# Householder steps below 128 in the form of the later ones: pieces in PSUM, an unmasked column for PE

## The chip, the core and the metric

The kernel runs on one core of one Trainium2 chip. The metric is the device time of one execution in microseconds, the median of several. All times stated here are microseconds unless marked ns.

## What is computed

Two residual layers on x (64 x 256 x 256), float32 throughout.

```python
# layer 0
h = relu(layernorm(x))                      # per batch element 256 nodes x 256 features
h = relu((adj*adj) @ (h @ W1))              # 256 -> 512
h = relu((adj*adj) @ (h @ W2))              # 512 -> 1024
x = x + (adj*adj) @ (h @ W3)                # 1024 -> 256
# layer 1
deg = adj.sum(0) + adj.sum(1) - diag(adj)
L_norm = d[:, None] * (diag(deg) - adj) * d[None, :]     # d = deg ** -0.5
_, U = eigh(L_norm)                         # once, 256 x 256
h = relu(layernorm(x))
x = x + U @ (relu((U.T @ h) @ W1 + b1) @ W2 + b2)
```

## The kernel before

The work falls into three parts. The batch is taken in 32 pairs of two elements for layer 0. Beside it runs the eigenvalue problem of the 256 x 256 matrix `A`: a reduction to tridiagonal form by 254 Householder steps, then bisection and eigenvectors on VectorE. Layer 1 follows when `U` is there.

`A` lies in SBUF as two blocks of 128 rows (`A[:, 0, :]`, `A[:, 1, :]`). A Householder step k takes column k of `A`, makes a reflector from it and updates the columns from k + 1 on (`rest`), 255 - k of them. Steps 0 to 127 involve both blocks of rows and are written by `householder`; from 128 on only the lower block is left, and `householder_one` writes them. The order of every engine is written out by hand, and the engines signal each other by counting semaphores. One step of `householder` goes like this:

- PE turns the masked column `xc` (two blocks) into a row that stands in all 128 partitions of the PSUM bank `p_x` (`step_x`, recorded on L1365). Below I call this turn X.
- VectorE copies the row to SBUF (`xr`, L874). It multiplies `A` by it and sums (L877, result `pc`). ScalarE meanwhile squares and sums `xr` (L611) and takes the root (L613).
- From the root VectorE makes `beta` (L882 to L888), then `qcol` (L890), `h_` (L892), the reflector `v` (L893), and after the reciprocal of `h_` the scaled `vn` (L900), `qn` (L902) and the negated inverse (L903). GpSimd saves `beta` and `v` (L460, L461).
- PE turns `qcol` into the row `p_q` (`step_q`, L1365 too). I call this turn Q.
- VectorE makes the first `col` (L906), the sum of a product (L909), the first update of either block of `A` (L865), `w` (L914), the second `col` (L918), which is the next column complete, the second update of block 0 (L869), the mask `xc` (L923), which lets PE go on, and the second update of block 1.

`householder_one` does the same for one block and differs in form: it subtracts where the other adds, its `beta` has one operation instead of two after the reciprocal but each of them waits for the one before, its second update reads the row where PE left it in PSUM (alternating `ps[0]` and `ps[2]`), and PE turns `col` itself: the mask follows behind the second update, for `v` of the next step. All of VectorE's operations count up `house_v`, HOUSE = 22 a step, and `done(i)` waits until i of the step have ended.

Between the turns X and Q, and between Q and the next X, PE does the matrix products of a pair of layer 0. `GROUPS` says which pairs go with how many steps: pairs 0 to 3 take 11 steps each, pairs 4 to 17 take 12, pairs 18 to 20 take 14. `beside` spreads a pair's products over the steps, 0.54 of each step's share between X and Q. A group is a hardware loop over its pairs on PE, ScalarE and GpSimd. Step 128 falls on the beginning of pair 11. ScalarE evicts the products; in a step it does the square and the root first. GpSimd makes scalars of the layer norm, in steps 116 to 123 the sums of weights (`sum_of_weights`, L496) that pairs from 11 on need, and at the end of each pair two additions of x to the result (`add_x`, L487), 128x512 each.

## Time and profile before

| | |
|---|---|
| runs, median of 3 | 2407.68 us (2406.26 to 2408.15) |
| profiled execution | 2405.8 us |
| its span | 2404.1 us |
| PE busy | 2332.5 us, 97% of the span |
| VectorE busy | 1981.1 us, 82% |
| ScalarE busy | 1011.2 us, 42% |
| GpSimd busy | 858.2 us, 36% |
| chain that ended last | PE 70%, VectorE 24% |
| mean granted TensorE clock | 0.995 |

The steps 0 to 127 take the first 791 us of the span, the steps from 128 on the time up to 1421 us, and then VectorE's bisection follows. PE's busy share is that of operations whose ends are modelled and that overlap, so a short idle time between two of them is hardly seen in it; where PE loses time is better read from the distances between its turns. Rows of a timeline show the start, the duration, the engine, the line, the operation with its output and inputs, and in brackets the idle time before it and what ended it. DVE is VectorE, ACT is ScalarE, POOL is GpSimd, and PEld is the loading of weights on PE.

### The profile page before, as it was taken

The page shows a single profiled execution, that of the slowest core. Times are in us where ns is not written, and L with a number is a line of the kernel's source. Part 1 is how long each engine was busy: PE and PEld are TensorE (multiplying, and loading weights), DVE is VectorE, ACT ScalarE, POOL GpSimd, SP SyncE. Part 2 cuts the span into 40 slices and gives each one's busy share as a digit, 9 for nine tenths or more (in the row PEclk, how much of TensorE's full clock was granted, in tenths as well). Part 3 has the DMA queues.
Part 4 walks back from the last instruction along what each step waited for, and adds up shares of the span by engine and source line. Part 5 has one row for each costly group of instructions (what it writes and reads, how often), then busy time and mean ns, then how long its engine had stood idle before and what let it go on. Part 6 is the DMA issues. An engine that isn't in the chain of part 4 may idle for free.

```text
span 2404.1 us, 44229 instructions
## 1 busy us (share of the span) xinstructions
PE 2332.5 (97%) x11228; PEld 1920.7 (80%) x11228; DVE 1981.1 (82%) x10140; ACT 1011.2 (42%) x2428; POOL 858.2 (36%) x1582
## 2 busy tenths in 40 slices
PE   6999999999999999999999999999999997999999
PEld 4788877777887777888877778887788886889998
DVE  6888888888888888877788889799999994447776
ACT  3333333333333444444444444444444443235554
POOL 1111111111112554444444455445545444243332
PEclk9999999999999999999999999999999998999999
DMA  2000000000000000000000000000000001014443
GB/s 99 27 27 27 9 27 18 27 27 27 27 9 27 19 27 27 27 26 27 27 27 27 27 27 27 27 10 27 26 26 26 27 27 35 18 44 135 132 131 110
DMA packets 90001, 89.72 MB, mean 37 GB/s; under 512 B 5376, under 2 KB 89088, under 8 KB 89856
## 3 DMA queue, kind: packets, MB, share of 16 engines
q1 hardware_dynamic: 89856, 88.23, 11.5%
q14 instruction: 108, 0.88, 0.1%
q8 instruction: 37, 0.61, 0.1%
HBM read 54.66 MB, written 33.55 MB: 37 GB/s over the span
## 4 chain that ended last, share of the span: by engine, by line
PE 70%; DVE 24%; issue 2%; POOL 2%; ACT 2%; SPq 0%; DMA 0%; POOLq 0%; DVEq 0%; ACTq 0%
PE ps L1451 30%; PE ps L1423 25%; PE ps L1629 9%; DVE ps L1064 6%; PE ps L1365 4%; DVE ahead L1067 3%; DVE shared L1148 3%; DVE ps L1145 2%; DVE ahead L1043 2%; PE ps L1639 1%; DVE negs L1070 1%; POOL hid2T L518 1%; PE ps L1576 1%; DVE A L865 1%; DVE A L869 0%
## 5 line engine op out<-in xcount | busy, mean ns | idle before, releaser
L460 POOL COPY Eb<-sc 128x1 f32 (+1 forms) x254 | 46.7, 184 | 850.0 <-DVE v L893 614.1
L1423 PE MATMUL ps<-agg2T,w 128*128 128x256 f32 x1408 | 325.1, 380 | 0.5
L1451 PE MATMUL ps<-w,hid2T 128*128 128x256 f32 x1344 | 307.2, 381 | 11.8 <-ACT hid2T L671 11.8
L1451 PEld LDWEIGHTS ps<-w,hid2T 128*128 128x128 f32 x1344 | 247.9, 190 | 57.1 <-ACT hid2T L671 21.9
L1423 PEld LDWEIGHTS ps<-agg2T,w 128*128 128x128 f32 x1408 | 257.8, 190 | 33.2 <-ACT agg2T L650 3.3
L611 ACT ACTIVATE squares<-xrow_sb 128x256 f32<-128x256 f32 (+5 forms) x128 | 47.7, 372 | 432.3 <-DVE xrow_sb L874 432.3
L1064 DVE RECIPROCAL ps<-ahead 128x40 f32<-128x40 f32 (+1 forms) x768 | 218.4, 331 | 0.1
L1451 PE MATMUL ps<-w,aggT 128*128 128x512 f32 x336 | 151.9, 597 | 13.1 <-ACT aggT L664 13.1
L1423 PE MATMUL ps<-w,hid2T 128*128 128x256 f32 x704 | 162.9, 379 | 0.0
L1451 PE MATMUL ps<-agg2T,w 128*128 128x256 f32 x672 | 156.0, 379 | 0.0
L1451 PE MATMUL ps<-hid2T,xin 128*128 128x256 f32 x672 | 155.5, 380 | 0.0
L487 POOL TENSOR_TENSOR xr<-xr,res 128x512 f32<-128x512 f32 x64 | 84.8, 1325 | 193.5 <-ACT res L664 171.5
L1451 PE MATMUL ps<-weightT,hid 128*128 128x256 f32 x672 | 152.1, 379 | 0.0
L1067 DVE SCALAR_TENSOR_TENSOR ahead<-ps,ne,ahead 128x40 f32<-128x40 f32 (+1 forms) x768 | 147.2, 224 | 0.0
L1451 PEld LDWEIGHTS ps<-weightT,hid 128*128 128x128 f32 x672 | 125.8, 191 | 24.1 <-issue 8.7
L1423 PEld LDWEIGHTS ps<-w,hid2T 128*128 128x128 f32 x704 | 129.5, 190 | 15.3
L1451 PEld LDWEIGHTS ps<-hid2T,xin 128*128 128x128 f32 x672 | 125.4, 190 | 17.2
L1451 PEld LDWEIGHTS ps<-agg2T,w 128*128 128x128 f32 x672 | 124.6, 190 | 17.9
L664 ACT ACTIVATE hid2T<-ps 128x512 f32<-128x512 f32 x168 | 99.1, 590 | 82.8 <-PE ps L1451 82.6
L613 ACT ACTIVATE root_s<-root_s,tiny 128x1 f32<-128x1 f32 x254 | 74.8, 295 | 131.5 <-DVE prods L947 125.1
L1451 PEld LDWEIGHTS ps<-w,aggT 128*128 128x128 f32 x336 | 62.6, 192 | 78.5 <-issue 63.6
L671 ACT ACTIVATE hid2T<-hid2T 128x512 f32<-128x512 f32 x168 | 101.6, 623 | 33.6 <-POOL hid2T L518 31.2
(387 smaller groups left out, 5700.0 us busy)
## 6 DMA issues: line engine op xcount, KB each, us to landing
xl<-in_x_dram SPq DMA_DIRECT2D x64, 256.0 KB, 2.9
xr<-in_x_dram SPq DMA_DIRECT2D x64, 256.0 KB, 2.9
x_dram<-xr SPq DMA_DIRECT2D x64, 256.0 KB, 2.3
xin<-x_dram SPq DMA_DIRECT2D x64, 256.0 KB, 2.8
out_dram<-xin SPq DMA_DIRECT2D x64, 256.0 KB, 2.2
w<-in_L_gnn_W_dram SPq DMA_DIRECT2D x1, 2048.0 KB, 9.4
w<-in_L_gnn_W_dram SPq DMA_DIRECT2D x1, 1024.0 KB, 11.4
w<-in_L_gnn_W_dram SPq DMA_DIRECT2D x1, 512.0 KB, 4.1
```

Of the source, the lines that this page charges most:

```text
L487: pool.tensor_tensor(xres[:, j, :, :], xres[:, j, :, :], res[:, j, :, :], ALU.add).then_inc(x1_ready, 1)
L613: act.activation(root_s[:, 1:2], root_s[:, 0:1], ACT.Sqrt, bias=tiny[:, 0:1]).then_inc(root, 1)
L664: act.activation(dst.rearrange("p a n -> p (a n)"), ring[i % 4][:, :], ACT.Relu if stage == "hid" else ACT.Copy).then_inc(evac, 1)
L671: act.activation(block_, block_, ACT.Relu).then_inc(fin, 1)
L1043: ins = dve.tensor_tensor(piv[g % 2][:, 0:n, d, :], diag.unsqueeze(2).to_broadcast([P, n, W]), pts.unsqueeze(1).to_broadcast([P, n, W]), A ...
L1064: inverse_made[d] = at(dve.reciprocal(inverse[:, d, :], here[:, d, :]))
L1067: pivot_made[d] = at(dve.scalar_tensor_tensor(there[:, d, :], inverse[:, d, :], ne2[:, off:off + 1], there[:, d, :], ALU.mult, ALU.add))
L1148: dve.scalar_tensor_tensor(Qfb[:, i + 1, lane], inverse_at(i)[:, lane], ne2[:, off:off + 1], Qfb[:, i + 1, lane], ALU.mult, ALU.add).then_ ...
L1365: ins = pe.transpose(dst[:, P * b:P * b + P], col(b).to_broadcast([P, P]), ident[:, 0, 0:P])
L1423: ins = pe.matmul(dst, a, b, start=start, stop=stop)
L1451: ins = pe.matmul(dst, a, b, start=start, stop=stop)
L1629: ins = pe.matmul(dst, a, b, start=start, stop=stop)
```

## The change

The steps below 128 are written by a new `householder_two`, which is `householder_one` for two blocks. `at_row(p_here, i)` is a piece of two columns in the same PSUM bank as the row, behind its 256 columns. There lie the sums `p_` (was `pc`), `vh` (was `vn`), `w_` (was `w`) and the next masked column. The bank alternates with k, `ps[0]` for even k, `ps[2]` for odd k. PE turns `col` unmasked. `xr` is cleared at the start and its element k + 1 at the end of each step, so that the part before `rest` stays zero for ScalarE's square. The mask is made of two operations of one column, behind both second updates. Since the bank has to be known where a loop's body is written, an odd number of steps allows one pair a group, and the two groups of 11 steps become four. In `householder_one` only the masked column moves to PSUM.

```diff
-        GROUPS = [(0, 2, 11, 0.54), (2, 4, 11, 0.54), (4, 6, 12, 0.54), (6, 8, 12, 0.54), (8, 10, 12, 0.54),
-                  (10, 11, 12, 0.54), (11, 14, 12, 0.54), (14, 18, 12, 0.54), (18, 21, 14, 0.54)]
+        GROUPS = [(0, 1, 11, 0.54), (1, 2, 11, 0.54), (2, 3, 11, 0.54), (3, 4, 11, 0.54), (4, 6, 12, 0.54),
+                  (6, 8, 12, 0.54), (8, 10, 12, 0.54), (10, 11, 12, 0.54), (11, 14, 12, 0.54), (14, 18, 12, 0.54),
+                  (18, 21, 14, 0.54)]
...
+            def at_row(p_here, i):
+
+                return p_here[:, N + NB * i:N + NB * i + NB]
...
+                p_, vh, w_, x_next, x_now = (at_row(p_here, 0), at_row(p_here, 1), at_row(p_here, 2), at_row(p_here, 3),
+                                             at_row(p_last, 3))
...
+                def second_update(b):
+                    return dve.scalar_tensor_tensor(A[:, b, rest], p_here[:, rest], w_[:, b:b + 1], A[:, b, rest],
+                                                    ALU.mult, ALU.subtract)
...
+                at(dve.tensor_copy(xr[:, rest], p_here[:, rest]))
+                for b in range(NB):
+                    ins = dve.scalar_tensor_tensor(prods[:, b, rest], A[:, b, rest], 1.0, p_here[:, rest],
+                                                   ALU.mult, ALU.mult, accum_out=p_[:, b:b + 1])
...
+                done(4)
+                at(dve.tensor_scalar(twice, inv_len, square, length, ALU.mult, ALU.add))
+                done(5)
+                dve.wait_ge(v_saved, k + 1)
+                at(dve.tensor_scalar(beta, twice, half, None, ALU.mult))
...
+                at(dve.tensor_scalar(vh, v[:, :], inv_h, None, ALU.mult))
+                dve.wait_ge(q_ready, k + 1)
+                at(dve.tensor_scalar(qn[:, :], qcol[:, :], inv_h, None, ALU.mult))
+                done(11)
+                dve.wait_ge(qrow, k + 1)
+                at(dve.scalar_tensor_tensor(prods[:, NB - 1, rest], p_q[:, rest], inv_h, xr[:, rest],
+                                            ALU.mult, ALU.mult, accum_out=uq))
+                at(dve.scalar_tensor_tensor(col[:, :], vh, p_q[:, here:here + 1], A[:, :, here], ALU.mult, ALU.subtract))
+                done(14)
+                at(first_update(0))
...
+                done(16)
+                dve.scalar_tensor_tensor(col[:, :], w_, head, col[:, :], ALU.mult, ALU.subtract).then_inc(col_ready, 1)
+                at(second_update(0))
+                done(17)
+                at(second_update(1))
+                dve.wait_ge(col_ready, k + 2)
+                for b in range(NB):
+                    ins = dve.tensor_scalar(x_next[:, b:b + 1], col[:, b:b + 1], below[:, b, here:here + 1], None, ALU.mult)
+                at(ins)
+                at(dve.memset(head, 0.0), HOUSE - 20)
...
-            def step_x(k, bl, s):
+            def step_x(k, bl, bank):
                 pe.wait_ge(col_ready, k + 1)
-                row(p_turn[s % 2] if len(bl) == 1 else p_x, lambda b: (col if len(bl) == 1 else xc)[:, b:b + 1], bl).then_inc(xrow, 1)
+                row(bank, lambda b: col[:, b:b + 1], bl).then_inc(xrow, 1)
```

VectorE, from the sum of the product to the copy of the next step, in step 0 before:

```order
L906 SCALAR_TENSOR_TENSOR col<-vn,ps,A 128x2
L909 SCALAR_TENSOR_TENSOR prods,sc<-ps,sc,xrow_sb 128x255
L865 SCALAR_TENSOR_TENSOR A<-ps,vn,A 128x255
L914 SCALAR_TENSOR_TENSOR w<-vn,sc,qn 128x2
L865 SCALAR_TENSOR_TENSOR A<-ps,vn,A 128x255
L918 SCALAR_TENSOR_TENSOR col<-w,xrow_sb,col 128x2
L869 SCALAR_TENSOR_TENSOR A<-xrow_sb,w,A 128x255
L923 TENSOR_TENSOR xc<-col,below 128x2
L869 SCALAR_TENSOR_TENSOR A<-xrow_sb,w,A 128x255
L874 COPY xrow_sb<-ps 128x256
```

and the same stretch now:

```order
L913 SCALAR_TENSOR_TENSOR prods,sc<-ps,sc,xrow_sb 128x255
L915 SCALAR_TENSOR_TENSOR col<-ps,A 128x2
L876 SCALAR_TENSOR_TENSOR A<-ps,A 128x255
L919 SCALAR_TENSOR_TENSOR ps<-ps,sc,qn 128x2
L876 SCALAR_TENSOR_TENSOR A<-ps,A 128x255
L922 SCALAR_TENSOR_TENSOR col<-ps,xrow_sb,col 128x2
L880 SCALAR_TENSOR_TENSOR A<-ps,A 128x255 x2
L928 TENSOR_SCALAR ps<-col,below 128x1 x2
L930 MEMSET xrow_sb 128x1
L885 COPY xrow_sb<-ps 128x254
```

The first `col` has gone behind the product, the mask from between the two second updates to behind them, and a clearing has come in before the next copy. PE waits for L923 before and for L922 now.

VectorE, from the root to `qcol` in the same step before:

```order
L882 RECIPROCAL sc<-root_s 128x1
L884 TENSOR_TENSOR sc<-root_s,sc 128x1
L885 TENSOR_TENSOR sc<-root_s,sc 128x1
L888 SCALAR_TENSOR_TENSOR sc<-sc 128x1
L890 SCALAR_TENSOR_TENSOR qcol<-A,sc,pc 128x2
```

and now:

```order
L892 RECIPROCAL sc<-root_s 128x1
L894 TENSOR_SCALAR sc<-sc,root_s 128x1
L897 TENSOR_SCALAR sc<-sc 128x1
L899 SCALAR_TENSOR_TENSOR qcol<-A,sc,ps 128x2
L900 TENSOR_SCALAR sc<-ps,sc 128x1
```

One operation is gone from this stretch, and each of those left reads the result of the one before.

## Rows read from the trace of the kernel before

**Rows 1.** Waits of the whole span: engine, line, waited for; total us, times, longest.

```profile
PEld ps L1365 <- DVE xc L923: 41.9, 76, 1.2
```

**Rows 2.** Timeline of PE: turns Q and X, 11-step pair, then 12-step pair.

```profile
246.73 0.38 PE L1365 MATMUL ps<-ident,qcol 128*128 128x128 f32 x2
...
249.54 0.38 PE L1365 MATMUL ps<-ident,xc 128*128 128x128 f32 x2
...
252.79 0.38 PE L1365 MATMUL ps<-ident,qcol 128*128 128x128 f32 x2
...
615.58 0.38 PE L1365 MATMUL ps<-ident,xc 128*128 128x128 f32 x2
...
618.83 0.38 PE L1365 MATMUL ps<-ident,qcol 128*128 128x128 f32 x2
...
621.20 0.38 PE L1365 MATMUL ps<-ident,xc 128*128 128x128 f32 x2
```

**Rows 3.** Timeline of VectorE and PE's turns: the step k = 54.

```profile
357.74 0.43 PE L1365 MATMUL ps<-ident,xc 128*128 128x128 f32 x2
358.28 0.38 DVE L874 COPY xrow_sb<-ps 128x212 f32<-128x212 f32 x1 [0.25 <-PE ps L1365]
...
359.52 0.16 DVE L882 RECIPROCAL sc<-root_s 128x1 f32<-128x1 f32 x1
...
360.10 0.22 DVE L890 SCALAR_TENSOR_TENSOR qcol<-A,sc,pc 128x2 f32<-128x2 f32 x1
...
361.03 0.22 DVE L902 TENSOR_SCALAR qn<-qcol,sc 128x2 f32<-128x2 f32 x1
361.03 0.38 PE L1365 MATMUL ps<-ident,qcol 128*128 128x128 f32 x2
...
361.52 0.23 DVE L906 SCALAR_TENSOR_TENSOR col<-vn,ps,A 128x2 f32<-128x2 f32 x1 [0.22 <-PE ps L1365]
...
362.81 0.21 DVE L918 SCALAR_TENSOR_TENSOR col<-w,xrow_sb,col 128x2 f32<-128x2 f32 x1
362.94 0.42 DVE L869 SCALAR_TENSOR_TENSOR A<-xrow_sb,w,A 128x201 f32<-128x201 f32 x1
363.28 0.16 DVE L923 TENSOR_TENSOR xc<-col,below 128x2 f32<-128x2 f32 x1
...
363.49 0.43 PE L1365 MATMUL ps<-ident,xc 128*128 128x128 f32 x2
```

**Rows 4.** Timeline at the end of a 12-step pair, step k = 55.

```profile
366.78 0.38 PE L1365 MATMUL ps<-ident,qcol 128*128 128x128 f32 x2
...
368.39 1.26 POOL L487 TENSOR_TENSOR xr<-xr,res 128x512 f32<-128x512 f32 x1 [1.55 <-ACT res L650]
368.56 1.11 DVE L918 SCALAR_TENSOR_TENSOR col<-w,xrow_sb,col 128x2 f32<-128x2 f32 x1
...
370.04 1.51 POOL L487 TENSOR_TENSOR xr<-xr,res 128x512 f32<-128x512 f32 x1 [0.38 <-ACT res L650]
370.14 0.43 PE L1365 MATMUL ps<-ident,xc 128*128 128x128 f32 x2 [0.81 <-DVE xc L923]
```

**Rows 5.** Timeline of VectorE and GpSimd in step 119.

```profile
741.01 1.27 POOL L496 TENSOR_TENSOR adj_sb<-w,xin 128x512 f32<-128x512 f32 x1
741.05 1.25 DVE L902 TENSOR_SCALAR qn<-qcol,sc 128x2 f32<-128x2 f32 x1
```

**Rows 6.** The masks, steps below 128 and from 128: durations min/median/max ns, first and last start.

```profile
L923 DVE TENSOR_TENSOR xc<-col,below x128: 147/158/1250, 32.2 to 791.2; 128x2 f32<-128x2 f32 x128
L985 DVE TENSOR_SCALAR xc<-col,below x126: 202/212/217, 796.7 to 1420.6; 128x1 f32<-128x1 f32 x126
```

**Rows 7.** Timeline of VectorE in step 128: reciprocal of the length, `qcol`.

```profile
792.86 0.16 DVE L953 RECIPROCAL sc<-root_s 128x1 f32<-128x1 f32 x1
...
793.62 0.27 DVE L960 TENSOR_SCALAR qcol<-A,sc,pc 128x1 f32<-128x1 f32 x1
```

**Rows 8.** Timeline of VectorE at the start: a clearing of one column.

```profile
0.87 0.06 DVE L816 MEMSET tiny<- 128x1 f32 x1 [0.87 <-PEq L1686]
```

**Rows 9.** Updates of 205 columns by form, 336 to 350 us: total us, mean ns.

```profile
L865 DVE SCALAR_TENSOR_TENSOR A<-ps,vn,A 128x205 f32<-128x205 f32 x2 | 0.9, 428 | 0.0
...
L869 DVE SCALAR_TENSOR_TENSOR A<-xrow_sb,w,A 128x205 f32<-128x205 f32 x2 | 0.8, 432 | 0.0
```

More of the change, by code:

```diff
@@ L371, in completed @@
             return [i for i, m in slot if m == (2 if UNITS[i][0] == "hid" else SIZE[UNITS[i][0]]) - 1]
+        for first, last, steps, _ in GROUPS:
+            assert last - first == 1 or steps % 2 == 0
         @block.sync
@@ L858, in at @@
                     ins.then_inc(house_v, n)
-                half, inv_len, h_, beta, inv_h, minus_inv_h, scaled, uq = (sc[:, i:i + 1] for i in range(1, 9))
+                half, inv_len, h_, beta, inv_h, _, twice, uq = (sc[:, i:i + 1] for i in range(1, 9))
                 square, length = root_s[:, 0:1], root_s[:, 1:2]
-                head = xr[:, here:here + 1]
+                head, top = xr[:, here:here + 1], p_here[:, here:here + 1]
+                p_, vh, w_, x_next, x_now = (at_row(p_here, 0), at_row(p_here, 1), at_row(p_here, 2), at_row(p_here, 3),
+                                             at_row(p_last, 3))
@@ L879, in householder @@
                 at(ins)
-                at(dve.tensor_scalar(half, head, 0.0, 0.5, ALU.is_ge, ALU.subtract))
+                at(dve.tensor_scalar(half, top, 0.0, 0.5, ALU.is_ge, ALU.subtract))
                 dve.wait_ge(root, k + 1)
                 at(dve.reciprocal(inv_len, length))
-                done(3)
-                at(dve.tensor_tensor(scaled, length, half, ALU.mult))
-                at(dve.tensor_tensor(uq, square, half, ALU.mult))
+                done(4)
+                at(dve.tensor_scalar(twice, inv_len, square, length, ALU.mult, ALU.add))
@@ L895, in householder @@
-                done(8)
-                at(dve.tensor_scalar(head, head, beta, None, ALU.add))
                 at(dve.reciprocal(inv_h, h_))
-                done(10)
+                at(dve.tensor_scalar(top, top, beta, None, ALU.add))
+                done(9)
                 dve.wait_ge(v_ready, k + 1)
-                at(dve.tensor_scalar(vn[:, b0:NB], v[:, b0:NB], inv_h, -1.0, ALU.mult, ALU.mult))
+                at(dve.tensor_scalar(vh, v[:, :], inv_h, None, ALU.mult))
                 dve.wait_ge(q_ready, k + 1)
-                at(dve.tensor_scalar(qn[:, b0:NB], qcol[:, b0:NB], inv_h, -1.0, ALU.mult, ALU.mult))
@@ L940, in householder_one @@
                 head, top = xr[:, here:here + 1], p_here[:, here:here + 1]
-                x_, v_, vh, w_, q_, qh, col_, p_ = (t[:, b:NB] for t in (xc, v, vn, w, qcol, qn, col, pc))
+                v_, vh, w_, q_, qh, col_, p_ = (t[:, b:NB] for t in (v, vn, w, qcol, qn, col, pc))
+                x_now, x_next = at_row(p_last, 3)[:, b:NB], at_row(p_here, 3)[:, b:NB]
                 done(0)
@@ L984, in householder_one @@
                 dve.wait_ge(col_ready, k + 2)
-                at(dve.tensor_scalar(x_, col_, below[:, b, here:here + 1], None, ALU.mult), HOUSE - 17)
+                at(dve.tensor_scalar(x_next, col_, below[:, b, here:here + 1], None, ALU.mult), HOUSE - 17)
+            link(dve.memset(xr[:, :], 0.0))
+            link(dve.tensor_tensor(at_row(p_turn[1], 3), A[:, :, 0], below[:, :, 0], ALU.mult))
             dve.wait_ge(house_v, 1)
-            dve.tensor_tensor(xc[:, :], A[:, :, 0], below[:, :, 0], ALU.mult).then_inc(col_ready, 1)
+            dve.tensor_copy(col[:, :], A[:, :, 0]).then_inc(col_ready, 1)
+            dve.wait_ge(col_ready, 1)
             for (first, last, steps, _), k0 in zip(GROUPS, FIRST_STEP):
@@ L1483, in _ @@
             for k in TAIL:
-                step_x(k, range(NB - 1, NB), k - TAIL[0])
+                step_x(k, range(NB - 1, NB), p_turn[k % 2])
                 step_q(k, range(NB - 1, NB))
```

59 lines of the change are left out of this document (16 added, 43 removed).

## Prediction

> **What bounds the kernel now.** I read the waits first, then PE's two row turns in each Householder step, then VectorE's part of one step. The longest thing PE's loads wait for in these steps is VectorE's masked column: 41.9 us in 76 waits [rows 1]. That is not the loss, since PE is often still multiplying while a load waits. The loss shows in the distances between the turns. I call the turn of the column X, the turn of `qcol` Q. In a step of an 11-step pair X to Q takes 3.25 us and Q to X 2.81 us [rows 2]; there PE is never short of work (both distances stay the same while VectorE's operations get narrower). In a 12-step pair the floor of the second distance is 2.37 to 2.38 us, as the narrow step near 618 us shows [rows 2], so PE's floors are 6.05 us a step in 11-step pairs and 3.25 + 2.37 = 5.62 in 12-step pairs. (k is the step; the width of the rest of A is 255 - k, 201 at k = 54.)
>
> At k = 54 a 12-step step takes longer than its floor: X to Q 3.29 (357.74 to 361.03) and Q to X 2.46 (361.03 to 363.49), in all 5.75 [rows 3]. The 0.08 in the second half is VectorE's chain, which ends with `xc`, 0.06 before PE's turn; the 0.05 in the first half is PE starting again after having stood still.
>
> The largest loss is at the end of each pair. There GpSimd adds x to the result (1.26 us and 1.51), and one VectorE operation that begins beside it takes 1.11 us instead of 0.21; Q to X is then 3.36 (366.78 to 370.14) [rows 4]. The longest `xc` is 1.25 where its median is 0.158 [rows 6]. The operations so stretched read two tensors from SBUF; those that read one of them in PSUM keep their length. In the steps 116 to 123 GpSimd sums weights, and there `qn`, two columns from SBUF to SBUF, takes 1.25 us; [rows 5] show one of the eight.
>
> **The change part by part.** k below 128 only; what PE multiplies for the features is the same.
>
> (1) **Ends of pairs.** With the pieces in PSUM, everything that VectorE does beside GpSimd's addition has at most one SBUF tensor: both kinds of update, the column steps, the products. The mask is now 128x1; this form in the later steps has a maximum of 217 ns over 126 executions, although GpSimd makes the same additions there [rows 6]. I take the stretch as gone. Each of the seven 12-step ends loses 3.36 - 2.38 = 0.98 now, plus the 0.05 of the restart. The excess shrinks with the width, since the chain that the stretch is added to shortens, to about 0.8: 7 x 0.97 = 6.8 us. In the four 11-step ends the stretch of 1.25 - 0.16 = 1.09 is added to a chain that has 0.3 to spare (2.81 against 2.5 of VectorE): 4 x 0.85 = 3.4. Together 10.2 us. Bounds: 0, if another operation is caught, and 10.5.
>
> (2) **The column reaches PE earlier.** Now from the start of the second `col` operation to PE's turn: 363.49 - 362.81 = 0.68 [rows 3]. After the change nothing stands between: its 0.21 and 0.06 of signal, 0.27. Against this, the first `col` now follows the product sum and the first update waits for it: 0.23 + 0.04 in place of an issue gap of 0.14, so +0.13. Net 0.28 at 202 columns. Q to X by VectorE becomes 2.46 - 0.28 = 2.18, under PE's 2.38. Ordinary 12-step steps so lose 0.08 + 0.05 at k = 54; by three width-dependent operations at 1 ns a column the 0.08 was 0.11 at k = 44 and is gone at about k = 81. A mean of 0.105 over some 32 steps is 3.4 us. In the second step of each pair PE has less work in the second half and waits for VectorE in all pairs: 10 x (0.25 + 0.05) = 3.0 us.
>
> (3) **VectorE's own loop gets longer**, and this is what takes something back. Between copy and `qcol`: the reciprocal to `qcol` takes 0.58 now (359.52 to 360.10) and 0.76 in the form that is taken over (792.86 to 793.62) [rows 3, 7], +0.18. After the last column operation two updates, two masks and a clearing of `head` must end before the next copy: 0.13 + 2 x 0.34 for the updates, 2 x 0.13 for the masks (the next operation starts 0.08 before the end of one, 362.94 + 0.42 to 363.28; a mask takes 0.212 [rows 6]), 0.06 for the clearing [rows 8], 0.04 for its signal: 1.17. The loop at 202 columns: copy to `qcol` 1.82 + 0.18; `qcol` to `qn` 0.93 and 0.14 to the product sum; from there to the second `col` 1.29 + 0.13; then 1.17. In all **5.66 us**. Seven width-dependent operations make it 0.007 a step: 5.73 at k = 44, 5.62, the floor, at k = 60, and 6.03 at k = 1 against 6.05. So VectorE becomes the bound of about 17 steps by 0.055 in the mean: -0.9 us. In the second and fourth step of a pair PE waits for an eviction that ScalarE makes after the root, and so after the copy; the copy is up to 0.15 later in the first two 12-step pairs: -0.6 us.
>
> (4) **Steps 116 to 123.** `qn` is still a 128x2 operation from SBUF to SBUF and still begins 0.58 after `v`, some 0.04 behind GpSimd's sum [rows 5]. It stays stretched, so VectorE's loop is the bound in these steps, and its change counts in full: +0.18, +0.13, -0.06 (the negated inverse is gone), -0.09 (1.05 for the tail against 0.55 + 0.05 + 0.54 by way of PE at 136 columns). +0.16 in six of the eight: -1.0 us.
>
> (5) **PSUM as a place for operands.** An update that reads its row in PSUM takes 428 ns, one that reads it in SBUF 432, at 205 columns [rows 9]. Pointers and accumulators in PSUM are not in the trace for this form; I bound them by 0 and by the 0.013 us that small operations differ, and take 0.07 a step over the 30 or so in which VectorE is at or near the bound: -2 us (at 0.1 and 40 steps -4).
>
> The Trainium skill, "VectorE: DVE Perf Modes", section "The TRN2 errata — SBUF-src ops pay a fixed extra latency per instruction", has a table in which a VectorE instruction costs 58 cycles plus its width from SBUF and 120 from PSUM, 65 ns more at 0.96 GHz; it speaks against this change. By it the eight or so operations moved would cost 0.5 us a step. The pair of [rows 9] disagrees with it by its whole amount, and the sum goes by the rows.
>
> (6) **At nothing:** copies of `rest` only (a few ns); the products that no longer wait for the copy (the root on ScalarE is later, 359.52 being its end); the four single groups in place of two loops. PE is fed in the same order, and a first pass through new code has shown no gap where groups change already. The start (clearing `xr`, two small operations) lies under the wait for weights.
>
> Steps from 128 on only move `x` to PSUM; the mask there ends well ahead of PE's row. From the end of the reduction on VectorE's eigenvalue chain begins earlier by what was gained, and I see nothing that would hold it.
>
> **Sum:** 10.2 + 3.4 + 3.0 - 0.9 - 0.6 - 1.0 - 2 = 12.1 us. The profiled execution took 2405.8 us (span 2404.1), so it would be 2393.7; it lies 1.9 under the median of 2407.68, for which I say **2396 us**. Its own range is 2391 to 2401: the small costs in (5) at zero or twice, the tail of (3) 0.05 off either way.
>
> **The rivals.**
> - *`qn` escapes in steps 116 to 123.* 0.04 us decides it [rows 5], and if VectorE is first, GpSimd waits only for its 0.22. Then these steps fall from 6.03 to near 5.62, which is 3.6 us more: 2392. For it: the small margin. Against: all eight were caught, and the distance from `v` to `qn` stays. The Trainium skill, "SBUF — State Buffer", section "Who interferes with whom", says of the shared pair that the first to issue holds it for its whole instruction. Chance 0.15.
> - *The loop is 0.14 longer than I make it* (masks and clearing do not overlap, or a wait costs more). Then VectorE bounds 35 to 40 steps and the gain halves: 2402. Chance 0.12.
> - *The pair ends stay stretched*, because another operation is caught, the clearing or a mask. Then 10.2 us mostly stay lost: 2405. Against: rows of the later steps. Chance 0.07.
> - *VectorE's loop becomes the bound everywhere, and the kernel slower.* Place: from the second `col` to the next copy, and each operation with a piece in PSUM. With 0.3 us more a step the loop is 5.96 at 202 columns and 6.33 at k = 1; over the steps 1 to 40 and 44 to 100 that costs some 20 us against the gains of 14: about 2415. Below +0.23 a step it is no loss. For it: ten operations change place and two are added. The table of the Trainium skill cited under (5) would give +0.5 a step and some 30 us beyond this. Against: [rows 9]. Chance 0.07.
>
> The chances: forecast 0.59, the rivals 0.15, 0.12, 0.07, 0.07. What this kernel's measurement can tell from no change is about 0.2%, 4.8 us: faster means below 2402.9. The forecast and the first rival lie there, and so does a third of the second. Faster 0.78, same 0.15, slower 0.07. The range that leaves out the last rival and the far end of the first: 2390 to 2405.
>
> **What the new profile would show.** (1) right: no VectorE operation of 1.1 us or more at a pair's end, Q to X there 2.8 and 2.4. (2): PE's turn 0.27 after the second `col` begins. (3): copy-to-copy 5.73 at k = 44 and 5.62 from k = 60 on; a copy 0.7 to 0.8 after X where it was 0.54. (4): `qn` at 1.25 us eight times, steps of 6.1 to 6.2. Wrong would be: copy-to-copy over 6.05 in the first pairs, an update over 0.45 at 205 columns, or long operations elsewhere beside GpSimd.

## The result, and the profile after

| | before | after |
|---|---|---|
| median of 7 runs | 2407.68 us (2405.16 to 2409.19) | 2398.58 us (2395.62 to 2399.31) |
| profiled execution | 2405.8 us | 2395.62 us |
| its span | 2404.1 us | 2393.9 us |
| VectorE busy | 1981.1 us | 2016.5 us |
| chain that ended last, PE / VectorE | 70% / 24% | 61% / 30% |

The ratio is 0.996 with the 95% interval [0.9949, 0.9971], so the changed kernel is faster by some 9.1 us. I forecast 2396 (own range 2391 to 2401). The profiled execution was the fastest of its seven; its span is 10.2 us shorter, against the 12.1 of my sum.

The sum by kinds of steps, read from PE's turns in both traces (time before minus time after, added up over the steps named; a minus is a loss):

| steps | X to Q | Q to X | together |
|---|---|---|---|
| last of a pair, three of the 11-step pairs | 0.00 | 2.49 | 2.49 |
| last of a pair, all seven 12-step pairs | 0.1 | 6.5 | 6.5 |
| first step, six 12-step pairs | 0.34 | 0.26 | 0.60 |
| fifth to eleventh step, six 12-step pairs | 0.89 | 0.92 | 1.81 |
| second step, six 12-step pairs | -1.04 | 1.23 | 0.19 |
| third step, six 12-step pairs | -0.01 | 0.16 | 0.15 |
| fourth step, six 12-step pairs | -1.32 | 0.17 | -1.15 |
| second step, three 11-step pairs | -0.01 | 0.65 | 0.64 |
| third step, three 11-step pairs | -1.14 | 0.01 | -1.13 |
| 116 to 123 | -0.53 | -0.31 | -0.84 |
| all of pair 0 | -0.55 | 1.20 | 0.65 |
| the rest | | | 0.2 |

That is 10.1 us up to the turn of step 128. X of step 0 came 0.57 earlier. The copy of the last step, at 1416.78 before and at 1406.22 after, is 10.6 earlier, so the steps from 128 on kept the gain; 0.4 was lost behind them.

First the end of a pair, k = 55, in the kernel after: start, duration, engine, line, operation, and in brackets the idle time with what ended it.

```profile
362.61 0.38 PE L1374 MATMUL ps<-ident,qcol 128*128 128x128 f32 x2
...
364.22 1.27 POOL L491 TENSOR_TENSOR xr<-xr,res 128x512 f32<-128x512 f32 x1 [0.96 <-ACT res L654]
364.24 0.22 DVE L919 SCALAR_TENSOR_TENSOR ps<-ps,sc,qn 128x2 f32<-128x2 f32 x1
...
364.70 0.21 DVE L922 SCALAR_TENSOR_TENSOR col<-ps,xrow_sb,col 128x2 f32<-128x2 f32 x1
364.83 0.76 DVE L880 SCALAR_TENSOR_TENSOR A<-ps,A 128x200 f32<-128x200 f32 x2
...
364.99 0.41 PE L1374 MATMUL ps<-ident,col 128*128 128x128 f32 x2
```

GpSimd adds for 1.27 us from 364.22, and four operations of VectorE that begin beside it keep their length, where in [rows 4] the second `col` took 1.11. Q to X is 364.99 - 362.61 = 2.38 instead of 3.36.

Then an ordinary step, k = 54, VectorE and PE's turns, to be laid beside [rows 3]:

```profile
353.66 0.42 PE L1374 MATMUL ps<-ident,col 128*128 128x128 f32 x2
354.19 0.34 DVE L928 TENSOR_SCALAR ps<-col,below 128x1 f32<-128x1 f32 x2
354.53 0.06 DVE L930 MEMSET xrow_sb<- 128x1 f32 x1
354.62 0.37 DVE L885 COPY xrow_sb<-ps 128x201 f32<-128x201 f32 x1
...
355.86 0.16 DVE L892 RECIPROCAL sc<-root_s 128x1 f32<-128x1 f32 x1
...
356.61 0.22 DVE L899 SCALAR_TENSOR_TENSOR qcol<-A,sc,ps 128x2 f32<-128x2 f32 x1
...
356.95 0.38 PE L1374 MATMUL ps<-ident,qcol 128*128 128x128 f32 x2
...
359.05 0.21 DVE L922 SCALAR_TENSOR_TENSOR col<-ps,xrow_sb,col 128x2 f32<-128x2 f32 x1
...
359.33 0.42 PE L1374 MATMUL ps<-ident,col 128*128 128x128 f32 x2
```

PE's turn follows 0.28 after the second `col` begins (before 0.68). The reciprocal to `qcol` takes 0.75. The copy no longer waits for X in this step: it begins 0.96 after X (before 0.54), when VectorE's own tail of updates, masks and clearing is done. The step takes 5.67 instead of 5.75. From k = 60 on ordinary steps take 5.62, PE's floor.

Where the rest went is seen in the fourth step of a pair, k = 47, on PE and ScalarE. Before and after:

```profile
316.96 0.43 PE L1365 MATMUL ps<-ident,xc 128*128 128x128 f32 x2
...
317.50 0.38 DVE L874 COPY xrow_sb<-ps 128x212 f32<-128x212 f32 x1 [0.24 <-PE ps L1365]
...
318.61 1.07 ACT L650 ACTIVATE agg2T<-ps 128x512 f32<-128x512 f32 x2
...
319.25 1.56 PE L1423 MATMUL ps<-agg2T,w 128*128 128x256 f32 x6
...
320.64 0.38 PE L1365 MATMUL ps<-ident,qcol 128*128 128x128 f32 x2
```

```profile
313.24 0.43 PE L1374 MATMUL ps<-ident,col 128*128 128x128 f32 x2
...
314.22 0.37 DVE L885 COPY xrow_sb<-ps 128x208 f32<-128x208 f32 x1
...
314.63 0.38 ACT L615 ACTIVATE squares<-xrow_sb 128x212 f32<-128x212 f32 x1 [3.94 <-DVE xrow_sb L885]
...
315.14 0.29 ACT L617 ACTIVATE root_s<-root_s,tiny 128x1 f32<-128x1 f32 x1
...
315.34 1.06 ACT L654 ACTIVATE agg2T<-ps 128x512 f32<-128x512 f32 x2
...
315.97 1.56 PE L1432 MATMUL ps<-agg2T,w 128*128 128x256 f32 x6 [0.57 <-ACT agg2T L654]
...
317.37 0.38 PE L1374 MATMUL ps<-ident,qcol 128*128 128x128 f32 x2
```

ScalarE waits 3.94 us for the copy, makes square and root, and only then evicts `agg2T`, which PE needs to go on. In both kernels PE's products resume 1.75 after the copy (317.50 to 319.25, 314.22 to 315.97). But the copy stands 0.54 behind X before and 0.98 behind it now. X to Q grew from 3.68 to 4.13.

### The profile page after: what moved, and what is told of

Read it like the earlier page. It is cut to its first block, busy times and chain, and to the rows that moved or that the text cites. A ratio compares the mean times of both kernels' runs of the same rounds, so it can differ in the third digit from the quotient of the medians.

```text
span 2393.9 us, 43889 instructions
## 1 busy us (share of the span) xinstructions
PE 2327.7 (97%) x11228; PEld 1923.6 (80%) x11228; DVE 2016.5 (84%) x10270; ACT 1010.8 (42%) x2428; POOL 856.8 (36%) x1582
## 4 chain that ended last, share of the span: by engine, by line
PE 61%; DVE 30%; issue 3%; ACT 3%; POOL 2%; SPq 0%; DMA 0%; POOLq 0%; ACTq 0%; DVEq 0%
PE ps L1460 29%; PE ps L1432 17%; PE ps L1638 9%; DVE ps L1073 6%; DVE ahead L1076 3%; DVE shared L1157 3%; PE ps L1374 3%; DVE ps L1154 2%; DVE A L876 2%; DVE ahead L1052 2%; DVE A L880 1%; PE ps L1648 1%; DVE negs L1079 1%; POOL hid2T L522 1%; DVE prods L913 1%
## 5 line engine op out<-in xcount | busy, mean ns | idle before, releaser
L615 ACT ACTIVATE squares<-xrow_sb 128x212 f32<-128x212 f32 (+7 forms) x128 | 47.4, 370 | 425.7 <-DVE xrow_sb L885 425.2
L509 POOL TENSOR_TENSOR hid2T<-agg2T 128x512 f32<-128x512 f32 x42 | 54.5, 1298 | 172.0 <-ACT agg2T L668 172.0
```

The source lines that it names most:

```text
L509: pool.tensor_tensor(moving_sum(n), a, b, ALU.subtract).then_inc(turn_s, 1)
```

## The experiments

Times are medians; ratios stand against runs of the kernel before that were made beside them on the same chip (2407.78 to 2408.69). "After" stands at 2398.58, beside 2407.68 for before. A difference between an experiment and "after", or between two experiments of different rounds, so carries up to 1 us of doubt, by which the runs of the kernel before differed. Sums over kinds of steps are read from one trace each and do not have it, but the first pair varies from execution to execution (see the run of the single groups).

**Only w back in SBUF.**

```diff
-                p_, vh, w_, x_next, x_now = (at_row(p_here, 0), at_row(p_here, 1), at_row(p_here, 2), at_row(p_here, 3),
+                p_, vh, w_, x_next, x_now = (at_row(p_here, 0), at_row(p_here, 1), w[:, :], at_row(p_here, 3),
```

> After with one change: in the steps below 128 w stands in SBUF again, so the second column operation reads two tensors from SBUF, as it did before. Theory (the gain at the pair ends comes from w's place, which takes an operation beside GpSimd's addition out of its reach): the operation is stretched again at all eleven pair ends, the distance Q to X there is 3.3 to 3.4 us in 12-step pairs instead of 2.38 and up to 3.6 in 11-step pairs instead of 2.81, and the kernel takes about 10 us more than the changed one, 2408. Rival (the gain at the ends comes from the order and from the mask behind the updates): the ends stay at 2.4 and 2.8, the time at 2398.

Measured 2404.2, ratio 0.9983 [0.9974, 0.9992]: 5.6 us lost, about half of what I expected. The stretch is back at nine of the eleven ends. At k = 55:

```profile
367.63 1.27 POOL L491 TENSOR_TENSOR xr<-xr,res 128x512 f32<-128x512 f32 x1 [0.96 <-ACT res L654]
367.65 0.21 DVE L919 SCALAR_TENSOR_TENSOR w<-ps,sc,qn 128x2 f32<-128x2 f32 x1
...
368.11 0.80 DVE L922 SCALAR_TENSOR_TENSOR col<-w,xrow_sb,col 128x2 f32<-128x2 f32 x1
...
368.97 0.43 PE L1374 MATMUL ps<-ident,col 128*128 128x128 f32 x2 [0.41 <-DVE col L922]
```

The column operation ends at 368.91, with the addition (368.90). It lasts as long as the addition has still to go, here 0.80, and Q to X is 2.95. The last steps of the seven 12-step pairs lost 4.0 us, that of pair 0 lost 0.55, and the three other 11-step ends 0.55 together: at two of these the column began before the addition, at step 32 by 0.04 us, and kept its 0.21. So w's place is worth about half of the gain at the ends, 5.1 of 9.9 us. The other half at a 12-step end is the way from the column to the turn: 3.36 - 2.95 = 0.41 is just the difference between 0.68 and 0.27, since behind a stretched column nothing hides it. I had counted all of it as stretch.

**Before, with w in PSUM and a mask of two operations.**

```diff
+                w = p_q[:, N:N + NB]
...
-                dve.tensor_tensor(xc[:, b0:NB], col[:, b0:NB], below[:, b0:NB, here],
-                                  ALU.mult).then_inc(col_ready, 1)
+                for b in bl:
+                    ins = dve.tensor_scalar(xc[:, b:b + 1], col[:, b:b + 1], below[:, b, here:here + 1], None, ALU.mult)
+                ins.then_inc(col_ready, 1)
```

> Before with only two changes: w in the PSUM bank of Q's row, and the mask made by two one-column operations; the order, the masked turn, the additions, the old beta stay. Theory (the gain of the whole change is the pair ends alone, and what the earlier column won in the other steps was lost again in steps bound by evictions and by VectorE's own loop): about 10 us less than before minus 0.1 us for each of some 60 steps that wait for the longer mask, so 2400 to 2403, with Q to X of 2.5 at the 12-step ends. Rival (my forecast: the column's way to PE is worth some 6 us of its own): the ends bring less than 10, and the time is 2404 or more.

Measured 2422.79, ratio 1.006 [1.0046, 1.0074]: slower than before by 14 us. Neither expectation had a loss in it; the rival's "2404 or more" covers the number and not how it came about. The end k = 55:

```profile
372.29 1.27 POOL L487 TENSOR_TENSOR xr<-xr,res 128x512 f32<-128x512 f32 x1 [1.54 <-ACT res L650]
372.46 0.21 DVE L919 SCALAR_TENSOR_TENSOR col<-ps,xrow_sb,col 128x2 f32<-128x2 f32 x1
372.59 1.19 DVE L870 SCALAR_TENSOR_TENSOR A<-xrow_sb,ps,A 128x200 f32<-128x200 f32 x1
373.71 0.32 DVE L925 TENSOR_SCALAR xc<-col,below 128x1 f32<-128x1 f32 x2
373.94 1.27 POOL L487 TENSOR_TENSOR xr<-xr,res 128x512 f32<-128x512 f32 x1 [0.38 <-ACT res L650]
373.95 1.48 DVE L870 SCALAR_TENSOR_TENSOR A<-xrow_sb,ps,A 128x200 f32<-128x200 f32 x1
```

The column operation is free, but the second update of block 0, which still reads row and `A` from SBUF, is caught in its place, and that of block 1 beside the second addition. Q to X is 3.40, and the copy of the next step comes later as well (copy to copy 7.53 there, 6.65 before). The ends of the three 11-step pairs did come free (2.49 us won, as in the changed kernel). The longer mask stands on PE's path and costs 0.17 in the ordinary 12-step steps up to some k = 73 (Q to X 2.63 for 2.46 at k = 54), not the 0.1 that I had put in, and less as the floor comes near, nothing at k = 114. By the trace the ordinary 12-step steps lost 6.5 us, the first steps of pairs, into which the stretched updates run over, 3.3, second steps 2.1, the steps 116 to 123 1.4, and pair 0 3.1. So w in PSUM alone frees nothing at the 12-step ends; the update from PSUM belongs to it. That the ends alone hold the gain is neither borne out nor refuted by this run.

**Only the old beta.** After the reciprocal two products that are independent of it, and one operation:

```diff
-                done(4)
-                at(dve.tensor_scalar(twice, inv_len, square, length, ALU.mult, ALU.add))
+                done(3)
+                dve.tensor_tensor(scaled, length, half, ALU.mult)
+                at(dve.tensor_tensor(twice, square, half, ALU.mult))
...
-                at(dve.tensor_scalar(beta, twice, half, None, ALU.mult))
+                at(dve.scalar_tensor_tensor(beta, inv_len, twice, scaled, ALU.mult, ALU.add))
```

> After with beta made as before: two products that don't wait for the reciprocal, then one operation, so 0.18 us less from the reciprocal to qcol (0.58 for 0.76). Theory (VectorE's loop from copy to copy is the bound where a step follows one that was short on PE: steps 46 to 59, the second and fourth step of 12-step pairs, the third of 11-step pairs, steps 116 to 123): each of those steps gets up to 0.18 us shorter, in all 4 to 6 us, 2393 to 2395. Rival (PE or the evictions are the bound there, the late copy only follows): under 1.5 us, 2397 to 2398.6.

Measured 2395.98, ratio 0.9948 [0.9934, 0.9961]: 2.6 us, between the two. Copy to copy at k = 48 to 55 falls from 5.69 to 5.65 down to 5.60 to 5.63, which confirms that VectorE's loop was the bound there. But a loop that is shorter by 0.18 wins just the 0.04 to 0.09 up to PE's floor. Steps 116 to 123 gave 0.88, fourth steps 0.53, second steps 0.28. One pair, that from step 68, got 0.23 longer; why VectorE's first product after Q of step 68 began 0.35 late stays open.

**Evictions ahead of the root**, on ScalarE:

```diff
+                        if s in (1, 2, 3):
+                            for i in completed(work_beside[s - 1][1]):
+                                evacuate(t, i)
                         step_root(k, columns(k0))
-                        for i in completed(work_beside[s - 1][1]) if s else []:
+                        for i in completed(work_beside[s - 1][1]) if s > 3 else []:
                             evacuate(t, i)
```

> After with one change on ScalarE: in the second, third and fourth step of a pair the eviction of the unit that PE completed before X is made ahead of the square and root of the step, not behind them. Theory (in these steps PE stands still in the first half for an eviction that waits for the root, and the root for the copy): PE no longer waits, X to Q falls from 3.97 to 4.49 in second steps and from 3.5 to 4.1 in fourth ones to about 3.3, VectorE's loop is then the bound there, and some 10 us go: 2388 to 2390. Rival (the eviction in front makes the root late by up to its 0.5 us): these steps stay as long as they are, 2398.

Measured 2389.63, ratio 0.9924 [0.9911, 0.9938]: 9 us faster than after. The same fourth step, k = 47:

```profile
311.22 0.43 PE L1377 MATMUL ps<-ident,col 128*128 128x128 f32 x2
311.39 0.60 ACT L654 ACTIVATE agg2T<-ps 128x512 f32<-128x512 f32 x1 [1.13 <-PE ps L1435]
...
312.20 0.37 DVE L888 COPY xrow_sb<-ps 128x208 f32<-128x208 f32 x1
...
312.61 0.38 ACT L615 ACTIVATE squares<-xrow_sb 128x212 f32<-128x212 f32 x1 [0.62 <-DVE xrow_sb L888]
...
314.51 0.39 PE L1377 MATMUL ps<-ident,qcol 128*128 128x128 f32 x2
```

The eviction begins 0.17 behind X, and ScalarE is idle again for 0.62 before the copy gives it the square, so the root isn't later. X to Q falls from 4.13 to 3.29. Six second steps gave 3.3 us, six fourth steps 3.5, the third steps of three 11-step pairs 1.1.

**The same order of evictions in the kernel before.**

> Before with the one change on ScalarE: evictions of units completed before X ahead of the square and root in steps two to four of a pair. Theory (PE waits in these steps for evictions behind the root, in both kernels): X to Q falls from 4.10 to 3.3 in second steps of 12-step pairs and from 3.68 to 3.3 in fourth ones, some 8 us in all, 2399 to 2401; the pair ends keep their stretched operation, Q to X 3.36. The distance to the changed kernel with the same order of evictions (2389.6) is then 10 us, the pair ends alone. Rival (the order of evictions pays only where the copy is late, in the changed kernel): 2406 to 2409.

Measured 2403.75, ratio 0.998 [0.9971, 0.9989]: 4.9 us, not 8, since the second steps only fell from 4.10 to 3.70. What matters is the pair of runs. With evictions first in both, the change is worth 2403.75 - 2389.63 = **14.1 us** instead of 9.1, and by the traces:

| steps | after against before | the same with evictions first in both |
|---|---|---|
| last of a pair, without pair 0 | 9.0 | 9.2 |
| second steps, six 12-step pairs | 0.19 | 1.38 |
| fourth steps, six 12-step pairs | -1.15 | 0.26 |
| third steps, three 11-step pairs | -1.13 | -0.04 |
| 116 to 123 | -0.84 | -0.99 |
| all up to step 127 | 10.1 | 14.0 |

The three middle rows differ by 3.7 us: that is what the steps that wait for an eviction took back. My theory of this run, that the distance would be the ends alone (10 us), fell: the earlier column is worth some 4 us beyond them once nothing takes it back.

**PE turns the masked column again**, all else as after. In the steps below 128:

```diff
-                dve.scalar_tensor_tensor(v[:, :], ident[:, :, here], beta, x_now, ALU.mult, ALU.add).then_inc(v_ready, 1)
+                dve.scalar_tensor_tensor(v[:, :], ident[:, :, here], beta, xc[:, :], ALU.mult, ALU.add).then_inc(v_ready, 1)
...
-                dve.scalar_tensor_tensor(col[:, :], w_, head, col[:, :], ALU.mult, ALU.subtract).then_inc(col_ready, 1)
+                dve.scalar_tensor_tensor(col[:, :], w_, head, col[:, :], ALU.mult, ALU.subtract).then_inc(col_made, 1)
                 at(second_update(0))
+                dve.wait_ge(col_made, k + 1)
+                dve.tensor_tensor(xc[:, :], col[:, :], below[:, :, here], ALU.mult).then_inc(col_ready, 1)
...
                 done(17)
                 at(second_update(1))
-                dve.wait_ge(col_ready, k + 2)
-                for b in range(NB):
-                    ins = dve.tensor_scalar(x_next[:, b:b + 1], col[:, b:b + 1], below[:, b, here:here + 1], None, ALU.mult)
-                at(ins)
...
-                row(bank, lambda b: col[:, b:b + 1], bl).then_inc(xrow, 1)
+                row(bank, lambda b: (xc if len(bl) == 2 else col)[:, b:b + 1], bl).then_inc(xrow, 1)
```

> After with one change: PE turns the masked column again. The mask is one operation of two columns into xc behind the second update of block 0, as before, and v reads xc; pieces in PSUM and the rest of the order stay. My forecast's price for this part was 0.41 us a step at the start and 6.4 us in all. Theory (the turn comes 0.41 us later, but VectorE's loop from copy to copy hides it where the loop is the bound, k = 44 to 59, and PE's floor hides it in 11-step pairs; it costs 0.05 to 0.2 a step from k = 60 to about 100, and in the second step of each pair): 3 to 5 us on the ordinary and second steps. The mask reads two tensors from SBUF and may be caught by GpSimd's addition at the pair ends, up to 0.9 a pair, which is a price of its own: 2402 to 2410 in all. Rival (the full 6.4 on the ordinary and second steps, as forecast): Q to X longer by 0.1 or more at k = 50 to 59 too.

Measured 2412.94, ratio 1.0018 [1.0009, 1.0027]: 14.4 us more than after, above the top of my expectation. The eleven ends cost 6.8 (the mask is caught at each, 0.53 at k = 55), first steps 1.3, ordinary steps 5.8, the steps 116 to 123 0.8, second and third steps of 12-step pairs 1.7, second steps of 11-step pairs 1.0; fourth steps and the third of 11-step pairs gave 1.7 back. The part was wrong in which I let the loop hide the later turn at k = 50 to 59: Q to X there is 2.60 to 2.56 and X to Q 3.29, 5.88 at k = 54 against 5.67. With the mask on its way, the loop that goes through PE is the longer one.

**A shorter tail**, all else as after:

```diff
                 done(17)
+                dve.wait_ge(col_ready, k + 2)
+                dve.memset(head, 0.0)
                 at(second_update(1))
-                dve.wait_ge(col_ready, k + 2)
-                for b in range(NB):
-                    ins = dve.tensor_scalar(x_next[:, b:b + 1], col[:, b:b + 1], below[:, b, here:here + 1], None, ALU.mult)
-                at(ins)
-                at(dve.memset(head, 0.0), HOUSE - 20)
+                at(dve.tensor_tensor(x_next, col[:, :], below[:, :, here], ALU.mult), HOUSE - 19)
```

> After with a shorter tail of VectorE's step: the mask is one operation of two columns instead of two of one, and the element head is cleared before the second update of block 1 instead of behind the mask. Theory (the time from the second col to the next copy counts in full where the loop is the bound): the loop gets 0.2 us shorter, steps 46 to 59 reach PE's floor of 5.62, the third step of 11-step pairs and the second and fourth of 12-step pairs lose up to 0.2 each, 2 to 4 us: 2395 to 2397. Rival (the mask has two inputs in SBUF again and is caught by GpSimd's addition at the pair ends): the copy of the next pair's first step comes up to 1 us later in some pairs, and nothing or less is won, 2398 to 2403.

Measured 2391.8, ratio 0.9931 [0.9918, 0.9945]: 6.8 us by the medians, more than expected; the two traces are 4.6 apart. Fourth steps gave 1.40, steps 116 to 123 1.42, second steps 0.91, the third of 11-step pairs 0.65, ordinary steps just 0.23. Once more the gain lies where something waits for the copy. The mask was caught at all eleven ends, as the rival had it, and took from 0.19 at k = 55 to 0.85 us at k = 43 instead of 0.16. But no turn of PE waits for the mask now, and it cost nothing that shows in them: Q to X there is 2.81 and 2.38 as after.

**p_ and vh in SBUF**, all else as after (`pc[:, :], vn[:, :]` for the first two pieces).

> After with p_ and vh of the steps below 128 in SBUF, w and the mask's result still in PSUM. It tells two things apart by classes of steps. First the price of pieces in PSUM, for which my forecast took 2 us: if they cost nothing, copy to copy at k = 46 to 59 stays 5.66 to 5.71; if they cost 0.07 a step, it is 5.6 to 5.64 there. Second the pair ends: w is now made from vh and qn, both in SBUF, and begins in GpSimd's addition (at 364.24, the addition at 364.22 in the changed kernel's trace), so by the theory of the shared port it lasts until the addition ends, 1.2 us, and Q to X at the 12-step ends is 3.2 to 3.4 instead of 2.38: 7 us more, 2405 to 2407. If only w's place matters at the ends, it stays 2398.

Measured 2400.3, ratio 0.9969 [0.9957, 0.9981]. The rows of two pair ends, k = 55 and k = 67:

```profile
366.75 1.26 POOL L491 TENSOR_TENSOR xr<-xr,res 128x512 f32<-128x512 f32 x1 [0.95 <-ACT res L654]
366.81 1.23 DVE L919 SCALAR_TENSOR_TENSOR ps<-vn,sc,qn 128x2 f32<-128x2 f32 x1
...
437.19 0.22 DVE L919 SCALAR_TENSOR_TENSOR ps<-vn,sc,qn 128x2 f32<-128x2 f32 x1
437.23 1.31 POOL L491 TENSOR_TENSOR xr<-xr,res 128x512 f32<-128x512 f32 x1 [1.02 <-ACT res L654]
```

It is the same operation at both ends. Where it begins 0.06 behind the addition it takes 1.23, where it begins 0.04 ahead it takes 0.22, and then the addition is 0.04 longer. It was caught once only, so that the ends lost 1.0 us and not 7: at k = 67 and at the five ends behind it VectorE is ahead, by 0.04 to 0.31. In the changed kernel the operation with `vh` in PSUM began 0.02 behind the addition and took 0.22, as its rows at k = 55 show. One of two inputs moved decides it, as far as this one end shows. The Trainium skill, "SBUF — State Buffer", section "Who interferes with whom", says this: an instruction of VectorE with two SBUF inputs and a GpSimd instruction that reads SBUF exclude each other, and the first to issue holds the shared port to its end. The rows agree on who is stretched. They don't show the addition held up for the whole of VectorE's operation: that had 0.18 still to go at 437.23, and the addition was longer by 0.04.

For the price of PSUM: copy to copy at k = 50 to 52 is 5.72 with these pieces in SBUF, 5.67 to 5.68 in the changed kernel. These two pieces in PSUM cost nothing here; they save 0.04 a step. Of the others w cost nothing either (the run with w in SBUF has the same 5.67 to 5.68 there); the mask's result wasn't moved by itself.

**Three changes together**: evictions first, the old beta, and `qn` made by two operations of one column.

```diff
-                at(dve.tensor_scalar(qn[:, :], qcol[:, :], inv_h, None, ALU.mult))
+                for b in range(NB):
+                    ins = dve.tensor_scalar(qn[:, b:b + 1], qcol[:, b:b + 1], inv_h, None, ALU.mult)
+                at(ins)
```

> After with three changes together: evictions ahead of the root in steps two to four of a pair, beta in the old form (0.18 us less from the reciprocal to qcol), and qn made by two one-column operations. Theory: the first alone gave 2389.6; with it VectorE's loop bounds steps 45 to 59, so the old beta now gives 0.05 to 0.1 in some 15 of them and up to 0.18 in second steps, about 2.5 us; the one-column qn isn't stretched beside GpSimd's sums in steps 116 to 123, which fall from 6.2 to about 5.65, 4.4 us: 2382 to 2384. Rival (one of the two columns of qn is still caught, as the addition of 1.27 us covers both): steps 116 to 123 stay at 6.0 to 6.2, 2386 to 2388.

Measured **2383.52**, ratio 0.9893 [0.9878, 0.9909]. The `qn` operations over the whole trace, after and then here (durations min/median/max in ns, first and last start):

```profile
L910 DVE TENSOR_SCALAR qn<-qcol,sc x128: 218/219/1265, 29.7 to 778.4; 128x2 f32<-128x2 f32 x128
```

```profile
L915 DVE TENSOR_SCALAR qn<-qcol,sc x256: 200/204/214, 29.9 to 764.9; 128x1 f32<-128x1 f32 x128
```

None is stretched, though GpSimd's sums are as they were, and steps 118 to 127 take 5.62 to 5.67. Against evictions first alone, steps 116 to 123 gave 4.46 us (expected 4.4) and the others 1.3 together (expected 2.5).

**Four together**, with the shorter tail too.

> The three changes together of the last run and the shorter tail as well. The shorter tail alone was worth 7 us where the copy was late in steps that wait for evictions. Theory (with evictions ahead of the root and the old beta, X to Q is at PE's floor of 3.25 and Q to X at 2.38 in nearly all steps, so VectorE is no bound any more): within 1 us of the three together, 2382.5 to 2384.5. Rival (VectorE's loop still holds back some steps): 2380 to 2382.

Measured 2383.08, ratio 0.99 [0.9885, 0.9915], 0.4 under the three, which is within the spread of either. The tail that was worth 6.8 us alone (4.6 by the traces) is worth 0.1 up to step 128 here. The three together had already taken the ordinary steps to PE's floor, 5.62 or 5.63, all but k = 77 and 78, which stay at 5.70 and 5.67 in both runs.

**The four single groups alone, in the kernel before.**

> Before with one part of the change alone: the first four pairs as four groups of one pair in place of two loops over two. Theory: at nothing, the median within 1.5 us of before, pairs 0 to 3 as long as before to 0.1 us. Rival (code that is met for the first time holds PE or ScalarE up at the start of each single group): the pairs from step 11 and from step 33 are longer by 0.3 us or more each.

Measured 2409.37, ratio 1.0001 [0.9992, 1.001]. The pairs from step 11 and 22 are as long as before to 0.06 us; that from step 33 is 0.80 shorter, as its last mask wasn't caught, and that from step 44 is 0.63 longer, since the update behind that mask was caught instead (1.48 us at 299.31). The grouping costs nothing that can be measured. Pair 0 took 79.3 us here, 77.06 before, 76.42 after and 75.8 to 80.2 in the other runs, while the pairs behind it, where the edit doesn't touch them, repeat to 0.1: the start of the kernel is where executions differ.

## Why the prediction was right, step by step

The time lies in the range and near the number, but two mistakes of the sum cancelled each other in part.

(1) **Ends of pairs: right.** 10.2 forecast; 9.0 plus 0.9 of pair 0 measured, Q to X 2.81 and 2.38 at all eleven, no VectorE operation of 1.1 us there. The mechanism was right too: the run with w in SBUF brings the stretch back at nine ends, that with `vh` in SBUF at one. That it needs all the pieces together I had said ("at most one SBUF tensor"), and the run on the kernel before shows that one of them alone only hands the stretch on.

(2) **The column reaches PE earlier: right in the operation, too high in the sum.** From the second `col` to the turn 0.28 (forecast 0.27), Q to X by VectorE 2.20 and 2.17 in the second steps k = 45 and 57 (forecast 2.18 at 202 columns). Ordinary 12-step steps, the first, third and fifth to eleventh, won 2.56, against 3.4 less the 0.9 of (3): as forecast, if the 2 of (5), which were laid on such steps too, are left out. Second steps won 1.9 in Q to X, with the one of pair 0 2.2 (forecast 3.0).

(3) **This is the step that failed.** VectorE's loop itself was right to 0.04: copy to copy 5.71 at k = 46 and 5.69 at k = 48 (forecast 5.73 at k = 44; there it read 5.95, since the copy still came 0.49 behind X and Q came at PE's floor of 3.24), 5.66 at k = 54, 5.62 at k = 60, and `qcol` 0.75 behind the reciprocal. Wrong was the sentence on steps that wait for an eviction: "the copy is up to 0.15 later in the first two 12-step pairs: -0.6 us". I compared the copy with the copy, and not with X. In a second step PE has less work, so X comes early, and I booked that as a gain under (2), while VectorE's loop held the copy, and with it root and eviction, where they were. At k = 47 the copy is 0.98 behind X, 0.44 later than before. The term was 3.7 us in the pairs from step 11 on by the comparison of kernels with evictions first, some 4 with pair 0, instead of 0.6. So at k = 45 the step took 6.60 before and 6.60 after, with X to Q 4.39 for 4.11 and Q to X 2.20 for 2.50.

(4) **Steps 116 to 123: right.** `qn` was caught eight times, at 1.25 to 1.26; 0.84 lost, 1.0 forecast.

```profile
743.16 1.27 POOL L500 TENSOR_TENSOR xin<-xin,w 128x512 f32<-128x512 f32 x1
743.20 1.26 DVE L910 TENSOR_SCALAR qn<-qcol,sc 128x2 f32<-128x2 f32 x1
```

The margin is again 0.04, as in [rows 5].

(5) **PSUM operands: forecast -2, nothing measured.** I had bounded the cost by 0 and 4 us, and the lower bound held. The run with two pieces in SBUF has the longer loop. The table of the Trainium skill, "VectorE: DVE Perf Modes", section "The TRN2 errata — SBUF-src ops pay a fixed extra latency per instruction", would have made it 0.5 us a step, and the loop shows nothing of that. Single operations do: the one-column operation in front of the reciprocal takes 199 ns in the kernel after, where it reads the row in PSUM, and 149 before, where it reads the copy in SBUF (medians of 128), and the read-out of an accumulator is longer too (last section). Both stand in front of the reciprocal, which waits for ScalarE's root.

(6) **At nothing: right**, shown for the groups. Steps from 128 on are as long as before to 0.1 us in all. The 0.4 that was lost behind them I didn't follow up.

So (3) took 3.4 more than forecast and second steps gave 0.8 less, (5) gave 2 more than forecast. That makes 9.9 of the 12.1, and the span fell by 10.2. That the time came so near to 2396 is owed in part to these 2 us, which were no more than a guess within bounds. The median fell by 9.1 only, since the profiled execution of after lies 3.0 under its median and that of before 1.9.

One of the signs that I had named for (3), the copy 0.7 to 0.8 behind X, read 0.92 to 0.98 at k = 46 to 59 (0.80 and 0.87 behind the fourth step, at k = 48 and 49) and 0.74 at k = 60: the difference pointed at the step that failed. I had named the value and not asked who else waits for the copy. Another sign, copy to copy over 6.05 in the first pairs, was no use as a sign: it was over 6.05 at the start of these pairs before the change too (6.34 at k = 12, 6.45 after), and in nearly all their other steps it stayed at 6.05.

## What to carry to other kernels

When a chain is shortened, ask which of its points each engine waits for. An earlier signal to one engine (PE's turn) is a gain only for what depends on it alone; what hangs on a later point of the same engine's loop (here the copy, then the root, then the eviction) stays, and the distance between the two comes back as a wait.

An in-order engine that waits for a late result should first do what is ready: ScalarE stood idle for 3.9 us with a finished product behind the root in its queue. Taking the eviction first was worth as much as the whole change, 9 us. Where VectorE and GpSimd work side by side, free every operation of the stretch from a second SBUF tensor, not just the one that is seen to be caught, or move it to where nothing waits for it: the mask in the shorter tail was caught eleven times and cost no turn anything.

## What the runs showed of the hardware

- Reading VectorE's accumulator into PSUM takes longer than into SBUF, before and after:

```profile
L877 DVE DVE_READ_ACCUMULATOR prods<-A,xrow_sb x256: 76/83/86, 18.8 to 786.3; 128x1 f32 x128
```

```profile
L887 DVE DVE_READ_ACCUMULATOR prods<-A,ps x256: 136/141/144, 18.1 to 776.3; 128x1 f32 x128
```

  That is 58 ns, twice a step. The input moved as well between the two, from the copy to the row in PSUM. With the sum back in SBUF and the input still in PSUM (the run with p_ and vh in SBUF) it is the old figure, so it is where the sum goes that counts:

```profile
L887 DVE DVE_READ_ACCUMULATOR prods<-A,ps x256: 80/83/86, 18.5 to 780.1; 128x1 f32 x128
```

  It costs nothing here, as the reciprocal behind it waits for ScalarE (355.86 at k = 54, 0.33 behind the start of the root).
- `qn`, one input and the result in SBUF, two columns, is caught by GpSimd's sum; the same operation made of two of one column never is (204 ns, 256 times, of which 16 began inside a sum, for instance one at 719.80 beside the sum of 719.76). An operation with one SBUF input can be caught as well, and splitting it is a cure.
- Less than 0.05 us decides who is caught, and the recorded starts don't tell it that finely. In all these traces every operation of VectorE with two SBUF tensors that began behind an addition of GpSimd, and 0.1 us or more before its end, was stretched. Of those that began up to 0.05 us ahead of it some escaped and five were stretched as well. The same operation at k = 127, in the kernel before and in the one with single groups:

```profile
789.83 0.21 DVE L918 SCALAR_TENSOR_TENSOR col<-w,xrow_sb,col 128x2 f32<-128x2 f32 x1
789.87 1.30 POOL L487 TENSOR_TENSOR xr<-xr,res 128x512 f32<-128x512 f32 x1 [1.76 <-ACT res L650]
```

```profile
791.53 1.32 DVE L918 SCALAR_TENSOR_TENSOR col<-w,xrow_sb,col 128x2 f32<-128x2 f32 x1
791.58 1.27 POOL L487 TENSOR_TENSOR xr<-xr,res 128x512 f32<-128x512 f32 x1 [1.75 <-ACT res L650]
```

  Both began 0.04 us ahead (0.05 in the rounded figures of the second); one took 0.21 us and the other 1.32. So a margin of this size, as at k = 67 with `vh` in SBUF, is not one to build on.
